# Sixteen-head attention phases: compact key and query products, head tiles filled by copies inside SBUF, and one run of units over all groups

## What is computed

```python
q, k, v = split_heads(LN(x) @ Wq + bq), split_heads(ctx @ Wk + bk), split_heads(ctx @ Wv + bv)
p = softmax(q @ k.T / sqrt(8))          # phase 4: with a mask on the keys
y = merge_heads(p @ v) @ Wo + bo        # phase 6: heads 8 to 15 on every second token,
                                        # their output interpolated back to 128 tokens
```

## Time and profile before

| | |
|---|---|
| three runs | 1005.93, 1010.61, 1012.45 us; median 1010.61 |
| the profiled execution | 1011.52 us, of which the span is 1009.7 us |
| TensorE busy | 907.7 us, 90% of the span |
| VectorE, GpSimd, ScalarE busy | 572.8, 476.4, 442.1 us |
| mean granted TensorE clock | 0.946 |
| phase 4 | about 414.8 to 588 us |
| phase 5 | about 588 to 664.9 us |
| phase 6 | about 664.9 to 841 us |

### The profile page before, as it was taken

One profiled execution on the slowest core, in us unless ns is written; L12 is line 12 of the kernel. 1 busy time (PEld: TensorE's weight loads), 2 busy tenths in 40 slices (PEclk: granted clock), 3 DMA queues, 4 the chain that ended last, 5 costly groups with the idle time before them and its releaser, 6 DMA issues.

```text
span 1009.7 us, 13519 instructions
## 1 busy us (share of the span) xinstructions
PE 907.7 (90%) x4523; PEld 602.3 (60%) x4523; DVE 572.8 (57%) x1530; ACT 442.1 (44%) x777; POOL 476.4 (47%) x444
## 2 busy tenths in 40 slices
PE   5989898979899999898989967589899897999998
PEld 5866575656566666464655635355455455666664
DVE  6767454747446643457576556754756645663632
ACT  2334434445252423365656633336455464243321
POOL 3655646466536465535353303332533414756553
PEclk9899999999899999999999977779999997999999
DMA  8202201224032423000000030000000003243141
GB/s 321 84 2 84 74 11 53 84 91 137 31 111 74 132 96 93 0 2 1 2 1 1 1 133 1 0 1 2 1 2 1 1 1 107 82 148 103 71 149 62
DMA packets 32436, 59.28 MB, mean 59 GB/s; under 512 B 4880, under 2 KB 5264, under 8 KB 32112
## 3 DMA queue, kind: packets, MB, share of 16 engines
q1 hardware_dynamic: 32224, 58.42, 17.5%
q10 hardware_dynamic: 144, 0.01, 0.0%
HBM read 56.90 MB, written 1.51 MB: 58 GB/s over the span
## 4 chain that ended last, share of the span: by engine, by line
PE 59%; DVE 7%; ACT 4%; issue 3%; POOL 1%; DVEq 0%; ACTq 0%
PE Y L1040 11%; PE B L868 5%; PE B L870 5%; PE B L869 5%; PE B L1331 5%; PE B L1266 5%; PE B L1346 4%; PE B L1298 4%; PE B L1305 3%; PE B L1297 2%; PE Y L1361 1%; ACT shared L1393 1%; DVE shared_r L1473 1%; PE B L1271 1%; DVE shared_r L1475 1%
## 5 line engine op out<-in xcount | busy, mean ns | idle before, releaser
L1154 POOL TENSOR_TENSOR shared<-shared,bcs 128x512 f32<-128x512 f32 x192 | 245.8, 1283 | 221.2 <-DVE shared L1185 201.2
L1185 DVE TENSOR_TENSOR shared<-shared,B 128x512 f32<-128x512 f32 x204 | 139.4, 686 | 215.0 <-PE B L870 150.8
L1055 ACT ACTIVATE shared<-B 128x512 f32<-128x512 f32 x204 | 121.6, 598 | 284.6 <-PE B L870 284.4
L1040 PE MATMUL Y<-shared,down_lo 128*128 128x512 f32 x408 | 209.9, 602 | 0.0
L1451 POOL TENSOR_TENSOR shared_r<-shared_r,const 128x512 fp32r<-128x512 f32 (+1 forms) x128 | 126.2, 1018 | 141.9 <-DVE shared_r L1475 109.3
L1521 DVE TENSOR_REDUCE mxh<-B 128x4 fp32r<-128x512 f32 (+1 forms) x128 | 79.1, 620 | 63.4 <-PE B L1298 63.0
L1414 ACT ACTIVATE shared<-B 128x512 f32<-128x512 f32 (+1 forms) x128 | 69.7, 544 | 67.2 <-PE B L1305 66.6
L1040 PEld LDWEIGHTS Y<-shared,down_lo 128*128 128x128 f32 x408 | 73.5, 192 | 22.5 <-issue 11.2
L868 PE MATMUL B<-shared_r,gate_hi 128*128 128x512 f32 x102 | 82.8, 812 | 0.0
L868 PE MATMUL B<-x_lo,gate_hi 128*128 128x512 f32 x102 | 76.0, 745 | 0.7 <-ACT shared L1055 0.7
L1331 PE MATMUL B<-const,shared 128*128 128x128 f32 x448 | 73.6, 282 | 0.0
(11 more groups left out here) (288 smaller groups left out, 1719.0 us busy)
## 6 DMA issues: line engine op xcount, KB each, us to landing
bcs<-wrow SPq DMA_DIRECT2D x96, 256.0 KB, 3.6
bcs<-wrow SPq DMA_DIRECT2D x128, 128.0 KB, 3.0
gate_lo<-in_moe SPq DMA_DIRECT2D x9, 256.0 KB, 5.7
up_lo<-in_moe SPq DMA_DIRECT2D x9, 256.0 KB, 6.0
down_lo<-in_moe SPq DMA_DIRECT2D x9, 256.0 KB, 5.8
small<-in_small SPq DMA_DIRECT2D x1, 1378.5 KB, 10.6
X<-in_x SPq DMA_DIRECT2D x4, 256.0 KB, 5.4
CT<-in_ctx_t SPq DMA_DIRECT2D x4, 256.0 KB, 5.7
```

The lines of the kernel that those rows point to most:

```text
L1040: nc.tensor.matmul(Y[:], w_raw[2][:, at:at + P], hid[(n0 + c) % HIDDEN], start=(i == 0), stop=(i == m["NC"] - 1))\
L1055: nc.scalar.activation(sg[(n0 + n) % ACTIVE], B[n % GATES][:], ACT.Silu).then_inc(sem("sg_ready"), 1)
L1154: gp.tensor_tensor(hid[(n0 + n) % HIDDEN], hid[(n0 + n) % HIDDEN], bcs[(PLACE.k0[p] + r // m["PER"]) % BROADCAST], ALU.mult)\
L1185: nc.vector.tensor_tensor(hid[(n0 + n) % HIDDEN], sg[(n0 + n) % ACTIVE], up[:], ALU.mult)\
```

## The change

1. Weights of key and query are no longer repeated: `Wq`, `Wk` are 128x128 and one product makes all 16 heads' keys of a group, one all queries ("compact"). ScalarE writes the high part (`comp_hi`), VectorE the low part (`comp_lo`).
2. The head tiles are filled by DMA from `comp_hi` and `comp_lo`: four copies of 32 partitions x 512 columns (64 KB) for each of the eight tiles, 32 a group, issued by SyncE (`heads_sp`). In a tile the rows are now ordered by copy, then head, then feature, and `rowmask` follows.
3. The units of all four groups run on in one loop of 64 (plus a drain). The next group's compact products, values, norm, and the previous group's last divisions, interpolation, transposes, output product and result are done in slots of the running units, one after another through bank `T`. `B[0:2]` belong to scores, `B[2:4]` to transposes, `B[4:6]` to the sums, for the whole phase.
4. `vh` and `vc` have two buffers; GpSimd fills the second at the start of the kernel. In phase 6 the values of heads 0 to 7 and of heads 8 to 15 are made apart, half as wide.
5. For the first quad of a phase, `k_each` is made by three engines: GpSimd one part, ScalarE one, VectorE two.

```diff
-    Wq4=(P, HEAD_TILES * P), Wk4=(P, HEAD_TILES * P), Wq6=(P, HEAD_TILES * P), Wk6=(P, HEAD_TILES * P),
+    Wq4=(P, P), Wk4=(P, P), Wq6=(P, P), Wk6=(P, P),
...
+        def back_at(q):
+            return GB * q + (10 if q % QUADS == 0 else 8)
...
+            def compact(g, kq, bank):
+                if kq == "q":
+                    pe.wait_ge(sem("xhat_t_ready"), s0 + g + 1)
+                mm(bank[:], S(f"W{kq}{p}"), context(g) if kq == "k" else xhat_t[g % 2][:], start=True, stop=True)\
+                    .then_inc(sem("compact_mm"), 1)
...
+            def score(u):
+                g, a, j, w = unit(p, u)
+                q = QUADS * g + a
+                if j == 0:
+                    pe.wait_ge(sem("heads_k_each"), eq + q + 1)
+                    if q == 0:
+                        pe.wait_ge(sem("heads_k_first"), 3 * (e // NG + 1))
+                    pe.wait_ge(sem(f"heads_q{a}"), 16 * COPIES * (e + g + 1))
+                if u >= 2:
+                    pe.wait_ge(sem("heads_es_ready"), eu + u - 1)
...
+            compact(0, "q", SC[0])
+            compact(0, "k", SC[1])
+            values(0, PV[0])
+            for n in range(NALL + 9):
+                g, t = divmod(n, NU)
+                if n < NALL:
+                    score(n)
+                if 0 <= n - 1 < NALL:
+                    shift(n - 1)
+                if g < NG and t == 0:
+                    next_rows(g)
+                if g + 1 < NG and t == 3:
+                    pe.wait_ge(sem("xhat_t_ready"), s0 + g + 2)
+                    compact(g + 1, "q", T)
+                if g > 0 and t == 6 and p == 6:
+                    upsample(g - 1)
+                if g > 0 and t == 7:
+                    heads_turned(g - 1)
+                if g > 0 and t == 8:
+                    output(g - 1)
+                if g + 1 < NG and t == 9:
+                    if g:
+                        pe.wait_ge(sem("heads_oT_ready"), e + g)
+                    else:
+                        pe.wait_ge(sem("compact_lo"), 2 * (e + 1) + 1)
+                    compact(g + 1, "k", T)
+                if g < NG and t == 11:
+                    result(g)
+                if g + 1 < NG and t == 13:
+                    pe.wait_ge(sem("x_updated"), s0 + g)
+                    values(g + 1, T)
...
+                if 0 <= n - 2 < NALL:
+                    turn(n - 2)
+                if 0 <= n - 3 < NALL:
+                    weigh(n - 3)
+                for q in (n // GB - 2, n // GB - 3):
+                    if 0 <= q < QUADS * NG and back_at(q) == n:
+                        back(q)
...
+            def high(g, kq, bank):
+                act.wait_ge(sem("compact_mm"), 2 * (e + g) + "qk".index(kq) + 1)
+                if g:
+                    act.wait_ge(sem(f"heads_{kq}{HEAD_TILES - 1}"), 16 * COPIES * (e + g))
+                nc.scalar.activation(comp_hi[kq][:], bank[:], ACT.Identity, bias=S(f"b{kq}{p}"))\
+                    .then_inc(sem("compact_hi"), 1)
...
+        def heads_sp(sp, p):
+            def query(g, a):
+                sp.wait_ge(sem("compact_hi"), 2 * (e + g) + 1)
+                sp.wait_ge(sem("compact_lo"), 2 * (e + g) + 1)
+                if g:
+                    sp.wait_ge(sem("heads_score_mm"), eu + NU * (g - 1) + GB * (a + 1))
+                for c in range(COPIES):
+                    part = comp_hi["q"] if c < 2 else comp_lo["q"]
+                    sp.dma_start(qh[a][32 * c:32 * (c + 1), :].bitcast(F32), part[32 * a:32 * (a + 1), :].bitcast(F32))\
+                        .then_inc(sem(f"heads_q{a}"), 16)
...
+            for g in range(NG):
+                if g == 0:
+                    query(0, 0)
+                    key(0, 0)
+                    key(0, 1)
+                    query(0, 1)
+                    key(0, 2)
+                else:
+                    query(g, 0)
+                    query(g, 1)
+                    key(g, 0)
+                    key(g, 1)
+                    key(g, 2)
+                query(g, 2)
+                key(g, 3)
+                query(g, 3)
...
+            def each(g, a):
+                q = QUADS * g + a
+                pool.wait_ge(sem(f"heads_k{a}"), 16 * COPIES * (e + g + 1))
+                if q >= 2:
+                    pool.wait_ge(sem("heads_score_mm"), eu + GB * (q - 1))
+                for i in (0,) if q == 0 else range(HEAD_TILES):
...
+            each(0, 0)
+            each(0, 1)
+            for g in range(NG):
+                each(g, 2)
+                each(g, 3)
+                if g + 1 < NG:
+                    power(s0 + g + 2)
+                    each(g + 1, 0)
+                    each(g + 1, 1)
...
+            low(0, "q", SC[0])
+            low(0, "k", SC[1])
+            values(0, PV[0])
+            norm_stats(st, 1)
+            dve.wait_ge(sem("heads_k0"), 16 * COPIES * (e + 1))
+            for i in (2, 3):
+                v.tensor_scalar(k_each[0][:, i, :], kh[0].bitcast(F32), K("rowmask")[:, i:i + 1], None, ALU.mult)\
+                    .then_inc(sem("heads_k_first"), 1)
+            apply(s0 + 1, range(GB))
...
+                if g + 1 < NG:
                     if t == 4:
+                        low(g + 1, "q", T)
+                    if t == 10:
+                        low(g + 1, "k", T)
+                    if t == 14:
+                        values(g + 1, T)
...
+                    if t == 8 and g < NG - 1:
+                        norm_stats(st, (g + 2) % NG)
+                    if t == 14 and g < NG - 1:
+                        apply(s0 + g + 2, (0, 1))
+                    if t == 15 and g < NG - 1:
+                        apply(s0 + g + 2, (2, 3))
...
+            heads_sp(sp, 4)
             sp.wait_ge(sem("y_ready"), STEP[5])
...
+            heads_sp(sp, 6)
...
+            gp.memset(vh[1][:], 0.0).then_inc(sem("lowest_ready"), 1)
+            gp.memset(vc[1][:], 0.0).then_inc(sem("lowest_ready"), 1)
```

More of the change, by code:

```diff
@@ L37 @@
 HEAD_TILES = 4
+COPIES = P // (HEAD_TILES * DK)
 VW = 32
@@ L1258, in heads_pe @@
             pe.wait_ge(sem("constb_loaded"), 16)
[L1259 to L1267, removed]
@@ new lines, in weigh @@
+            def weigh(u):
+                g, a, j, w = unit(p, u)
+                q = QUADS * g + a
+                pe.wait_ge(sem("heads_pt_ready"), eu + u + 1)
+                if u % NU == 0:
+                    pe.wait_ge(sem("heads_v_ready"), e + g + 1)
+                if j == 0 and q >= 2:
+                    pe.wait_ge(sem("heads_os_ready"), eq + q - 1)
+                heads = P // w
+                for i in range(0, HEAD_TILES, heads):
+                    if coarse(p, a):
+                        val = vc[g % 2][:, j * (HEADS // 4) + 2 * (a - 2) + i // 2, :]
+                    else:
+                        val = vh[g % 2][:, j * HEADS + 4 * a + i, :]
+                    ins = mm(PV[a % 2][VW * i:VW * (i + heads), j * w:(j + 1) * w], val,
+                             pt[u % 2][:, i // heads * w:(i // heads + 1) * w], start=True, stop=True)
+                ins.then_inc(sem("heads_pv_mm"), 1)
@@ new lines, in back @@
+            def back(q):
+                pe.wait_ge(sem("heads_os_ready"), eq + q + 1)
+                if q % QUADS == 0:
+                    pe.wait_ge(sem("ysb_ready"), s0 + q // QUADS)
+                else:
+                    pe.wait_ge(sem("heads_osb_ready"), eq + q)
+                for x in range(GB * width(p, q % QUADS) // P):
+                    ins = nc.tensor.transpose(Y[:, x * P:(x + 1) * P], os[:, x * P:(x + 1) * P], ident)
+                ins.then_inc(sem("heads_ob_mm"), 1)
@@ L1442, in heads_pool, with output, result @@
-        def heads_pool(pool, p, g, groups):
-            e = NG * (p // 2 - 2)
-            for a in groups:
+            def output(g):
+                pe.wait_ge(sem("heads_oT_ready"), e + g + 1)
+                mm(Y[:], S(f"Wo{p}"), oT[:], start=True, stop=True).then_inc(sem("y_ready"), 1)
+            def result(g):
+                pe.wait_ge(sem("ysb_ready"), s0 + g)
+                if g + 1 < NG:
+                    pe.wait_ge(sem("compact_lo"), 2 * (e + g + 2))
+                else:
+                    pe.wait_ge(sem("heads_oT_ready"), e + g)
+                for j in range(GB):
+                    ins = nc.tensor.transpose(T[:, j * P:(j + 1) * P], ysb[:, j * P:(j + 1) * P], ident)
+                ins.then_inc(sem("yt_ready"), 1)
@@ L1540, in build @@
+            for _ in pieces:
+                pass
         area5 = Area()
@@ L1806, in _ @@
                 elif p > 3:
-                    for g, _, after, h in stages(pool, p):
-                        s = STEP[p] + g
-                        heads_pool(pool, p, g, (0, 1))
-                        power(s + 1)
-                        heads_pool(pool, p, g, (2, 3))
+                    heads_pool(pool, p)
         @block.scalar
```

499 lines of the change are left out of this document (229 added, 270 removed).

## The result

The changed kernel takes 982.99 us (median of four runs, 978.87 to 987.25), the kernel before beside it 1011.53 us. The ratio is 0.9729, 95% interval 0.9671 to 0.9787. That is 28.5 us faster where 60 us were forecast, and outside the range of 935 to 974 us. The profiled execution took 981.14 us (span 979.4 us), 30.4 us less than that of before.

| stretch | before | after | gain | forecast |
|---|---|---|---|---|
| phases 0 to 3 | 414.85 | 409.46 | 5.4 | 0 |
| phase 4 | 172.1 | 154.8 | 17.3 | 29.5 |
| phase 5 | 78.0 | 79.2 | -1.2 | 0 |
| phase 6 | 173.9 | 164.3 | 9.6 | 30.3 |
| phase 7 | 170.9 | 171.6 | -0.7 | 0 |

What follows compares the result with a forecast made beforehand. TensorE's own work was taken to bound phases 4 and 6. Openings, three shorter periods and ends gain 29.5 us in phase 4 and 30.3 us in phase 6, together 59.8 us: from 1011.5 to 951 us, range 935 to 974 us.

Steps and rivals of the forecast that it cites:

- The sum for TensorE's work: Removed per group: products 5.4 us, seam waits 3.7 (phase 4) and 3.5 us (phase 6), low clock 1.7 us (phase 6).
- Bank T: In-order hand-overs between TensorE, ScalarE and VectorE: `result` in slot 11 waits about 0.7 us for the low part, both phases.
- `k_each` in phase 6: At each group's start TensorE waits 1.6 us for `k_each`, as the 9.1 us chain exceeds 7.5 us of room.
- Rival D: Copies limit by throughput and the kernel gets slower: at 1.6 us a copy, 1065 us; chance 0.03.
- What is added: waits of the new chain: Waits before the next group's first score and in slots: 0.8 us a period in phase 4, 2.8 us in phase 6.
- ScalarE and VectorE each lose more split work than they gain: In running groups of phases 4 and 6, claimed of the other engines' load; no added time counted.
- a clock of 1.00 inside phase 6: The granted clock stays at 1.00 there; before, 1.7 us were lost behind each seam.
- The openings: First maxima sooner at the start of phases 4 and 6: gains 3.1 and 3.7 us; TensorE starts at 1.2 GHz as before.
- The end of each phase is the same chain as before.: Ends of phases 4 and 6: nothing changes there, so no time was counted.
- The ends: Missing first drain and extra last drain cancel; the last group's seam gives 1.5 us, plus 1.7 us clock in phase 6.
- rival A: Copies land late, at 5.7 us: 21.6 us lost, waits bring back low clock, 10 us; 973 to 983 us; chance 0.2, shared.
- the steady period of phase 4: From first unit to first unit of successive groups: 33.6 us, where it was 41.9 us.

Runs made afterwards that it cites:

- run 12: Run 6 plus 60 (phase 4) and 48 (phase 6) transposes that nobody reads, filling TensorE's wait in the openings; 950.90 us, ratio 0.9366.
- Run 1: The changed kernel with two buffers each for the compact query's high and low parts; 975.45 us, ratio 0.9632 to the kernel before.
- Run 2: The changed kernel with VectorE's norm instructions moved from slots 14 and 15 to slots 11 and 12; 972.63 us, ratio 0.9618 to the kernel before.
- run 3: The changed kernel with VectorE's routing of phase 7 begun two slots later at phase 6's end; 984.35 us, ratio 0.9711 to the kernel before.
- run 5: The changed kernel with two query buffers, norm in slots 11 and 12 and later routing together; 957.43 us, ratio 0.9436 to the kernel before.
- run 6: Run 5 plus ScalarE issuing the first query tile's copies in each opening, so SyncE begins with the key's; 956.90 us, ratio 0.9436.
- run 11: Run 5 plus 73 (phase 4) and 53 (phase 6) transposes that nobody reads, filling the openings; 955.34 us, ratio 0.9395.
- run 7: The changed kernel with 82 (phase 4) and 54 (phase 6) transposes that nobody reads, filling TensorE's wait in the openings; 987.56 us, one run.

## Why the prediction was wrong

Phases 4 and 6 gained 26.9 us where 59.8 us were forecast. The 32.9 us that are missing lie here (the forecast's column is the one of before less the gains forecast for it):

| opening, three periods, last group to its output product | before | after | forecast | run 12 |
|---|---|---|---|---|
| phase 4 | 12.9, 125.7, 33.5 | 11.0, 106.4, 37.5 | 9.8, 100.8, 32.0 | 9.9, 98.0, 36.6 |
| phase 6 | 15.2, 123.0, 35.7 | 11.9, 109.0, 43.4 | 11.5, 99.6, 32.5 | 9.4, 92.6, 38.4 |

So 15.0 us are missing in the periods, 16.4 us in the last stretches and some 1.5 us in the openings.

**What held.** The sum for TensorE's work (six products, the waits and the low clock of the seam). Bank T: `result` waits 0.58 us in phase 4 and 0.41 us in phase 6 for the low part, 0.7 us forecast. `k_each` in phase 6: 0.31, 0.69 and 0.98 us against 1.6; its terms were off both ways (issue 0.63 instead of 0.48 us, landing 2.0 instead of 3.0 us, a multiplication 1.01 instead of 1.17 us). GpSimd's fills at the start cost nothing that shows. Rival D's throughput limit isn't near: 32 x 0.63 = 20 us of 35.

**The step that failed first** is "What is added: waits of the new chain". It followed the key forward to the next score, and only that. It left out the buffer's way back: `high` in slot 4 waits until the last copy of the earlier query has read `comp_hi`. I wrote that SyncE needs 15 of 33 us and stopped there. In the opening all 32 copies are issued from 412.1 to 432.6 us, when slot 4 of the first group is due at about 432 us. Run 1 prices it at 3.8 and 5.8 us in the first periods, 7.5 us of the time.

**The second:** "ScalarE and VectorE each lose more split work than they gain". Busy shares were right, durations were not: a norm instruction moved beside GpSimd's multiplications takes up to 1.15 instead of 0.34 us. I had asked only whether GpSimd would slow down. Run 2 prices it at 10 us, with the clock that falls behind the waits. The forecast of a clock of 1.00 inside phase 6 failed by these two steps and the next: the three periods had 0.79, 0.91 and 0.95.

**The third:** in "The openings" I wrote that TensorE would start at 1.2 GHz, as before, and counted nothing. But before, the first five units took 8.7 us (427.7 to 436.4) at a clock of 1.00 and 9.1 us at 0.81, after 11.2 us at 0.63 and 10.9 us at 0.59: behind the idle time of 8.2 us [against 2.83 us in rows 3] the clock stays low for longer. (It isn't always so in phase 4: in runs 3, 5 and 6, without a filling, they took 9.5 to 9.6 us.) Besides, the first maxima came 2.5 and 3.8 us sooner after the first product, not 3.1 and 3.7 us, and in phase 6 the query product, now first, waits 0.8 us for its normed rows, which is most of what phase 5 lost. With nothing behind that takes it back, a held clock is worth 3.6 us up to the end of phase 6's first period (runs 11 and 12).

**The fourth:** "The end of each phase is the same chain as before." In phase 6 it was not: with units running on, routing work came between the last quads and their divisions, 3.3 us (run 3). That is a small part of the 16.4 us missing in the last stretches. I had let two things cancel in "The ends": the first period lacks an earlier group's drain, the last group has one more. In phase 4 of run 12 the first period is 2.3 us shorter than the others (31.1 against 33.4 us), but the last stretch is 4.6 us over its forecast, and 5.9 us in phase 6. What the rest is stays open.

**The rivals.** 983 us lies where rival A ended, and that would be the wrong lesson: the copies landed sooner than forecast, after 2.0 us. The estimate of 2.15 us that I had worked out from the Trainium skill ("DMA: Bandwidth & Descriptors", section "Anatomy of one DMA"), whose figures are for the other issuing path, stood nearer than my row. Only the second half of rival A, waits that bring back the low clock, is what happened, behind other waits. With the four items mended phases 4 and 6 gain 172.1 - 144.5 = 27.6 us and 173.9 - 140.5 = 33.4 us, 61.0 us together, where 59.8 us were forecast, and the time is 950.9 us, as forecast. Part of that is luck. The last stretches are still 10.5 us over the forecast and the periods 9.8 us under it; the openings' clock is held and their copies are issued by two engines, which the forecast didn't have; and the gain in phases 0 to 3, which it put at nothing, makes up for a phase 5 that is 2.4 us longer and for a median that is 3.3 us above the trace. What the runs do bear out is the steady period of phase 4: 33.3 to 33.5 us with the norm moved, 33.6 us forecast.

## What to carry to other kernels

When work is moved off a bound engine by a buffer and copies, follow the buffer both ways: who needs the data, and who waits to write it again. Do it for the first group too, where all copies are issued at once. When an instruction is moved into another slot, look at what its neighbours do then: a VectorE instruction from SBUF to SBUF beside GpSimd can take three times as long. When an edit gives nothing, look whether the next wait grew by what it gained, and try it again once that wait is gone. When an edit is worth less than the spread of phases that it doesn't touch, read its own stretch in several traces and not the total time.

## What the runs showed of the hardware

- SyncE issues copies inside SBUF of 64 KB and 32 partitions every 0.63 us (2.51 us for four), where weight loads took 0.48 us; they land after 2.0 us (median), a few after up to 3.8 us.
- VectorE's 128x128 fp32 norm takes 0.34 us alone and up to 1.15 us beside GpSimd's multiplications; row maxima from PSUM don't change.
- A filling of TensorE that ended 2.27 us before the next real work left the clock at 0.61 over the next 8.8 us; ones that ended 0.19 us (run 7) and 1.27 us (run 11) before left it at 1.00 over the first five units.
- Five units took 8.5 and 7.9 us at a clock of 1.00 (run 7), 11.2 and 10.9 us at 0.63 and 0.59. Waits of 1.9 us in a period of phase 6 came with 2.7 us of longer work at the lower clock behind them (run 2).
- Phase 5, with the same work on every engine, took 79.1 to 85.4 us, as its mean granted clock went from 0.70 to 0.58.
